# Two-digit lookups with three one-hot pairs and three low-digit pairs in SBUF, where there were two and four

## What is computed

```
x = jnp.concatenate([ne[nums], fe[fr]], axis=-1)      # 11 features, tables of 1000 rows x 4
nwf = jax.vmap(enc)(nwf_num_emb[fm], nwf_freq_emb[fm], ..., nwf_numbers, nwf_freqs)
feats = jnp.concatenate([goby_emb[goby_idx], ..., m_from, m_to, ..., nwf], axis=-1)
return jax.nn.relu(feats @ reduce_W + reduce_b)
```

## Time and profile before

| what | value |
|---|---|
| median of 3 runs | 1870.71 us (1870.64 to 1873.35) |
| the profiled execution | 1870.87 us |
| its span, first to last instruction | 1869.1 us |
| PE busy | 1699.5 us (91%) |
| ACT busy | 1488.3 us (80%) |
| DVE busy | 1423.0 us (76%) |
| POOL busy | 929.2 us (50%) |
| DMA queue of SP, share of the 16 engines' span | 78.1% |
| mean granted PE clock | 0.969 |

### The profile page before, as it was taken

The page is one execution under the profiler, slowest core; times in us unless marked ns, Lnnn a source line. Parts: engine busy times, 40 slices in busy tenths (PEclk is TensorE's granted clock), DMA queues, the critical chain, the costliest instruction groups (busy, mean ns, idle before and its releaser), DMA issues.

```text
span 1869.1 us, 59759 instructions
## 1 busy us (share of the span) xinstructions
PE 1699.5 (91%) x25092; PEld 780.9 (42%) x25092; DVE 1423.0 (76%) x1279; ACT 1488.3 (80%) x2579; POOL 929.2 (50%) x476
## 2 busy tenths in 40 slices
PE   2157989999999999999999999999999999999995
PEld 2112434444444444444444444444444444444444
DVE  7056668888888788888888888887888888888871
ACT  3235768888888888888888888888888888898883
POOL 7435874445444444545444544545444544545442
PEclk9578999999999999999999999999999999999997
DMA  6696778888888888888888898888888888888831
GB/s 171 103 311 207 233 228 287 283 267 282 276 289 267 279 281 287 275 272 280 284 276 276 277 285 279 283 275 278 284 274 270 288 279 283 276 276 280 283 133 46
DMA packets 166154, 484.24 MB, mean 259 GB/s; under 512 B 53213, under 2 KB 104959, under 8 KB 120831
## 3 DMA queue, kind: packets, MB, share of 16 engines
q1 hardware_dynamic: 163327, 480.27, 78.1%
q0 software_dynamic: 2560, 0.15, 1.2%
HBM read 474.04 MB, written 6.09 MB: 257 GB/s over the span
## 4 chain that ended last, share of the span: by engine, by line
PE 73%; ACT 12%; issue 5%; POOL 1%; DMA 1%; DVE 1%; SPq 0%; DVEq 0%; POOLq 0%
PE ab L648 31%; PE e_ps L571 19%; PE f_ps L648 11%; ACT gate L688 9%; PE ab L598 8%; PE ab L535 3%; ACT tanh_c L688 1%; ACT f_ps L697 1%; ACT gate L697 1%; DMA last_h<-nwf_h 0%; PE e_ps L924 0%; POOL ig L718 0%; POOL small_rows L281 0%; DVE kept L583 0%; DMA low<-last_h 0%
## 5 line engine op out<-in xcount | busy, mean ns | idle before, releaser
L718 POOL TENSOR_TENSOR ig<-gate 128x1024 f32<-128x1024 f32 x192 | 410.8, 2140 | 842.6 <-ACT seq_x L542 568.3
L561 DVE TENSOR_SCALAR hot<-low,cst 128x4096 bf16<-128x4096 bf16 x352 | 451.4, 1283 | 170.4 <-PE e_ps L571 166.3
L571 PE MATMUL e_ps<-hot,tab 128*32 128x512 bf16 x8448 | 529.7, 385 | 26.4 <-DVE kept L583 26.2
L583 DVE SCALAR_TENSOR_TENSOR kept<-high,cst,e_ps 128x1024 f32<-128x1024 uint8 x352 | 449.1, 1276 | 28.8 <-PE e_ps L571 20.0
L648 PE MATMUL ab<-seq_h,seq_wh 64*64 64x512 f32 x3072 | 409.3, 592 | 0.0
L571 PEld LDWEIGHTS e_ps<-hot,tab 128*32 128x32 bf16 x8448 | 204.8, 97 | 409.3 <-issue 251.1
L745 POOL TENSOR_TENSOR seq_h<-gate,tanh_c 128x1024 f32<-128x1024 f32 x128 | 303.7, 2373 | 19.6 <-ACT tanh_c L688 19.6
L695 ACT ACTIVATE gate<-ab 128x1024 f32<-128x1024 f32 x256 | 262.9, 1027 | 17.6 <-PE ab L648 11.7
L688 ACT ACTIVATE tanh_c<-seq_c 64x512 f32<-64x512 f32 (+1 forms) x384 | 241.5, 629 | 12.8 <-DVE seq_c L731 9.7
L688 ACT ACTIVATE gate<-ab 64x512 f32<-64x512 f32 (+1 forms) x384 | 228.4, 595 | 11.5
L697 ACT ACTIVATE gate<-ab,nwf_bias 128x256 f32<-128x256 f32 (+1 forms) x384 | 147.4, 456 | 104.3 <-PE ab L648 100.2
(11 more groups left out here) (77 smaller groups left out, 1674.7 us busy)
## 6 DMA issues: line engine op xcount, KB each, us to landing
low<-low_digits SPq DMA_DIRECT2D x352, 1024.0 KB, 7.3
tok<-seq_tokens SPq DMA_DIRECT2D x128, 384.0 KB, 4.7
high<-high_digits SPq DMA_DIRECT2D x1408, 32.0 KB, 3.4
nwf_in<-in_r_nwf_numbers SPq DMA_DIRECT2D x1, 2816.0 KB, 13.8
nwf_in<-in_r_nwf_freqs SPq DMA_DIRECT2D x1, 2816.0 KB, 21.0
low_digits<-turned SPq DMA_DIRECT2D x8, 352.0 KB, 5.5
high_digits<-turned SPq DMA_DIRECT2D x8, 160.0 KB
low<-last_h SPq DMA_DIRECT2D x11, 64.0 KB
```

The lines of the kernel that those rows point to most:

```text
L561: nc.vector.tensor_scalar(hot[:, p % HOT_RING, :, :].rearrange("p u c -> p (u c)"), low[:, p % LOW_RING, :, :].rearrange("p u c -> p (u c) ...
L571: last = nc.tensor.matmul(e_ps[32 * g:32 * g + 32, i, :], tab[:, part, 2 * m + ty, :], hot[:, p % HOT_RING, i, g * CH:(g + 1) * CH], start ...
L583: nc.vector.scalar_tensor_tensor(out=kept[:, p % KEPT_RING, :, :].rearrange("p u c -> p (u c)"), in0=high[:, p % HIGH_RING, :, :].rearrang ...
L718: nc.gpsimd.tensor_tensor(ig[:, n % 2, cols], gates[0][:, n % 2, cols], gates[1][:, n % 2, cols], ALU.mult).then_inc(ig_ready, 1)
```

## The change

Two sizes change and nothing else. The loops follow them: the compares run three pairs ahead of the lookups where they ran two ahead, and the low digits are loaded three pairs ahead of the SP loop's own pair where they were loaded four ahead. The number of semaphores `low_here` falls with the ring. The two buffers together take as many bytes of SBUF as before: a pair takes 8192 bytes of a partition in either.

```
-LOW_RING, HIGH_RING, HOT_RING, KEPT_RING = 4, 5, 2, 4
+LOW_RING, HIGH_RING, HOT_RING, KEPT_RING = 3, 5, 3, 4
```

## The result

The changed kernel takes 1896.68 us (median of 4, 1888.24 to 1897.45) against 1871.07 us before: ratio 1.0124, 95% interval 1.0094 to 1.0154. On another chip it was 1.0084 (1.0066 to 1.0103), with 1895.11 against 1879.65 us. It is slower by about 1%.

The account below looks back on a forecast made before the run. The prediction took PE as the engine the others wait for, with loads and compares hidden. It summed 1871 + 23 (late low DMAs at 62 places) + 0 (the start) = 1894 us, 1.2% slower, range 1867 to 1930.

Parts of the forecast that it names:

- two places a step: Second compare of both seq cells ahead of nwf cells: low DMA lands in 8.2 us against 8.1 until need.
- the cover that was named for the first compares of nwf cells: DVE sits idle behind these compares for 2.54 us (PE's lookup) or 2.26 us (ACT), so lateness up to that costs nothing.
- both sides of that wait move by one pair: Compare and the lookup it waits for both move one pair, so none of DVE's 166.3 us wait for PE goes.
- The 23 us: Late low DMAs ahead of nwf cells: mean 0.37 us late at each of 62 places; bounds 0 and 93 us.
- the 8.2 us of room: Second compares of seq cells ahead of nwf cells: 8.1 us from low DMA issue to need, plus 0.1 us spare.
- No loss: Rival: low DMAs at the two places land 2.1 us ahead of need; 1871 us, within 0.2%; chance 0.30.
- the prediction's estimate: By the skill's figures, token load, low 5, high 5 and low 6 take 8.0 us; no low DMA late, 1871 us.
- The queue backs up: Rival: queueing grows, landings of 9.2 us, 1.0 late at each of the two places: +62, 1933 us; chance 0.20.
- Faster: Rival: at the start the token load comes 5 us earlier and the fourth low isn't missed: 1866 us; chance 0.12.

## Why the prediction was right

**The sign and the mechanism.** Forecast 1894 us, measured 1897. The step that carries it is the time from a low DMA's issue to its compare at two places a step, 8.1 us by the slots. Measured in the changed kernel's trace, the median there is 8.0 and 8.1 us. For the same DMAs of the kernel before it is 15.4 to 15.6. The issue order of the timeline above is the one derived from the slots. The run with the loads one place earlier in the queue shows that this time is the cause: the order of the queue alone returns nine tenths of the loss. And the steps without a late compare are as short as before.

**The places.** From the third step on, DVE waits for a low DMA at the second compare of the seq cells ahead of the nwf cells in 27 of 60 cases, 0.40 us in the mean at one place and 0.70 at the other, together 33 us. Of each such wait 0.35 us was a wait for PE before, so 27 x 0.35 = 9.5 us were not new: 24 us net, against 21.4 us by which these steps grew and 25.4 between the spans. The prediction had 23. The other compares of the step wait 6 us in all, and the cover that was named for the first compares of nwf cells was hardly called on.

**What did not go.** DVE's wait for PE ahead of compares went from 166.3 to 151.9 us only because the DMA took its place. The argument that both sides of that wait move by one pair was right, and the run with three hot buffers and compares two pairs ahead shows the counterpart: there the wait vanishes.

**What was luck in the size.** The 23 us came from landings that were to grow from 7.3 to 8.2 us, with one in four late by 1.5. Over the whole steady part they did not grow (min, median, max):

```profile
DMA to landing us min/median/max: 4.6/7.4/10.2
```

against 7.3 in the earlier trace rows. At the two places the trace tells 20 of the 60, with medians of 6.8 and 7.0 us, but these 20 are not typical: 6 of them were late, against 21 of the 40 others. A late compare starts as its DMA lands, so 41 of the 60 can be read. With them the median of all 60 lies between 7.0 and 8.0 us, which leaves the growth to 8.2 not borne out, and 15 of them took more than the 8.2 us of room. So one in four passed the limit as reckoned, by 0.8 us in the mean and not by 1.5, which is 12 us and not 23. Most of the other 12 us, some 9, have a cause that the prediction's sum does not contain: in 19 of the 60 cases the low DMA itself is issued 0.9 us or more later than reckoned, mostly as the four high DMAs ahead of it took up to 3.1 us to issue in place of 1.7, and then landings of under 8.2 us are late too. Nearly half of the cases are late, by 0.9 us net in the mean. One term was about twice too large and one was missing; that they add up to 23 was luck, while the place, the lead and the sign were not.

**The rivals.** "No loss" rested on a stack of bytes at 381 GB/s plus 1.8 us, by which no DMA at the two places would be late; 27 were. The Trainium skill ("DMA: Bandwidth & Descriptors", "Anatomy of one DMA"), with 436 GB/s and 2.0 us, gives the same answer by the prediction's estimate, and the trace does not agree with it either; the page states these two figures for DMAs issued by GpSimd, and these are issued by SP. "The queue backs up" (1933 us) did not come: the queue's share over the span fell, from 78.1% to 74.3%. "Faster" by the start did not either. The third step begins 1.7 us later than before, but two profiles of the kernel before differ by 5.1 us at this place, so the start shows no effect of either sign. That a third buffer has a use of its own was not among the rivals.

## What to carry to other kernels

The lead of a prefetch is the time from its issue to its need, and three things set it at once: how many buffers there are, how far ahead the consumer itself runs, and what stands ahead in the issuing queue. Reckon it place by place from the timelines, issue times included, and compare it with the upper half of the landings. At the places without spare time behind them, a ring of three was enough with a lead of 9.2 us and cost 1.2% with 8; at places where the consumer had time to spare, 7.4 to 7.7 us cost nothing. A consumer made to run further ahead takes its lead from the loads, while an extra output buffer with the distance left alone takes away a wait, which was worth 0.3% on the two chips where it was tried.

## What was not expected of the hardware

A broadcast DMA of 256 KB in rows of 2 KB took 1.3 to 1.4 us of the 16 DMA engines, by the sum of its packets in the two traces that have it; 1024 KB in rows of 8 KB take 2.75 at the rate of the earlier trace rows. Per byte that is about twice as much. (The share of the queue as a whole is no measure of this: with the same bytes it was 78.1% of 1869.1 us before and 74.3% of 1894.5 us after, 52 us less.) The issue of four high DMAs on SP, 1.7 us as a rule in the kernel before, took up to 3.1 us at the two places of the changed kernel. And the same kernel takes 1871 us on one chip and 1880 on two others; a part of it, 5.1 us in the two profiles taken, lies ahead of the third step.
